# First query tile left unscaled in a hybrid layer's attention part

## The reference

```python
def _rmsnorm(t, w):
    inv = jax.lax.rsqrt(jnp.mean(tf * tf, axis=-1, keepdims=True) + EPS)
    return (tf * inv * w).astype(t.dtype)
q = (x @ Wq.T).reshape(b, s, H, HD).transpose(0, 2, 1, 3)      # H = 32, HD = 128
k = (x @ Wk.T).reshape(b, s, HKV, HD).transpose(0, 2, 1, 3)    # HKV = 8, so 4 query heads share a key head
v = (x @ Wv.T).reshape(b, s, HKV, HD).transpose(0, 2, 1, 3)
q = _rmsnorm(q, q_norm_w); k = _rmsnorm(k, k_norm_w)
scores = jnp.einsum('bkgqd,bksd->bkgqs', qg, k) / math.sqrt(HD)
bias = jnp.where(rel > 0, NEG_INF, slopes[:, :, None, None] * rel)
attn = jax.nn.softmax(scores + bias[None], axis=-1)
out = jnp.einsum('bkgqs,bksd->bkgqd', attn, v)
return out.transpose(0, 2, 1, 3).reshape(b, s, H * HD) @ Wo.T
```

## Time and profile before

| | us |
|---|---|
| median of 3 runs | 2434.09 |
| lowest, highest | 2433.47, 2441.58 |
| the profiled execution | 2437.14 |
| its span, first to last instruction | 2435.8 |
| TensorE busy in the span | 2373.6 (97%) |
| VectorE, ScalarE, GpSimd busy | 1646.2, 1189.8, 800.6 |

### The profile page before, as it was taken

How to read it: one execution, slowest core, us unless ns; L and a number is a source line. 1 busy time by engine, 2 the same in 40 slices (tenths; PEclk the granted TensorE clock), 3 DMA queues, 4 the chain that set the end, 5 groups by cost and what they waited for, 6 DMA issues and landing times.

```text
span 2435.8 us, 40875 instructions
## 1 busy us (share of the span) xinstructions
PE 2373.6 (97%) x12810; PEld 2020.9 (83%) x12810; DVE 1646.2 (68%) x3961; ACT 1189.8 (49%) x3788; POOL 800.6 (33%) x1204
## 2 busy tenths in 40 slices
PE   6899999999999999999999999999999989999999
PEld 4577777788888888988989889889898878888887
DVE  7666664534277877777777777777777776565553
ACT  6433332233256666666666666666666562222112
POOL 5530343212034344444443444444434350011000
PEclk9899999999999999999999999999999999999999
DMA  4235458987830634535346335344462306555554
GB/s 144 98 134 188 185 206 293 347 334 285 313 122 31 259 118 158 213 147 198 151 173 231 121 153 212 143 183 173 169 238 92 113 19 232 195 208 185 193 193 156
DMA packets 86579, 444.85 MB, mean 183 GB/s; under 512 B 9496, under 2 KB 16664, under 8 KB 66656
## 3 DMA queue, kind: packets, MB, share of 16 engines
q1 hardware_dynamic: 85008, 440.78, 48.5%
q10 hardware_dynamic: 1360, 1.46, 0.2%
HBM read 342.59 MB, written 99.61 MB: 182 GB/s over the span
## 4 chain that ended last, share of the span: by engine, by line
PE 82%; DMA 7%; DVE 4%; POOL 3%; ACT 2%; issue 2%; SPq 0%; ACTq 0%; POOLq 0%; DVEq 0%
PE psum L801 70%; DMA stage<-in_wqkv 3%; PE psum L2639 3%; PE psum L2615 2%; DMA weff_s<-short_st 1%; DMA weff_q<-q_parts 1%; POOL rr L2414 1%; PE psum L2633 1%; POOL prob L2446 1%; PE psum L1793 1%; DVE cc L2489 1%; PE psum L1814 1%; POOL srstd L1184 1%; PE psum L1826 1%; ACT prob L2388 1%
## 5 line engine op out<-in xcount | busy, mean ns | idle before, releaser
L801 PE MATMUL psum<-qw,xs 128*128 128x384 f32 x2688 | 512.0, 340 | 1.7 <-DMA xs<-weff_x 1.7
L801 PEld LDWEIGHTS psum<-qw,xs 128*128 128x128 f32 x2688 | 462.3, 189 | 2.5 <-DMA xs<-weff_x 1.9
L2446 POOL TENSOR_SCALAR prob<-prob,rsum 128x128 f32<-128x128 f32 (+1 forms) x512 | 231.6, 468 | 613.3 <-DVE rsum L2548 608.2
L2388 ACT ACTIVATE prob<-biased,nmax 128x256 f32<-128x256 f32 (+1 forms) x512 | 227.3, 447 | 125.8 <-DVE nmax L2538 125.8
L801 PE MATMUL psum<-wo_h,oT_h 128*128 128x512 f32 x512 | 214.3, 419 | 0.2
L801 PE MATMUL psum<-wo_h,oT_l 128*128 128x512 f32 x512 | 202.7, 396 | 0.0
L801 PE MATMUL psum<-wo_l,oT_h 128*128 128x512 f32 x512 | 202.5, 395 | 0.0
L2334 ACT ACTIVATE squares<-cc 128x128 f32<-128x128 f32 x512 | 152.6, 302 | 52.6 <-DVE cc L2468 49.6
L2489 DVE TENSOR_TENSOR cc<-cc,rr 128x512 f32<-128x512 f32 x64 | 97.7, 1526 | 102.3 <-POOL rr L2414 102.3
L2414 POOL TENSOR_TENSOR rr<-ss,mneg_half 128x6 f32<-128x6 f32 (+1 forms) x128 | 150.3, 1174 | 10.7
L801 PE MATMUL psum<-xT0h,wgu 128*128 128x512 f32 x448 | 152.1, 399 | 0.0
(11 more groups left out here) (338 smaller groups left out, 5903.0 us busy)
## 6 DMA issues: line engine op xcount, KB each, us to landing
xs<-weff_x SPq DMA_DIRECT2D x62, 1792.0 KB, 7.9
wgu<-weff_gu SPq DMA_DIRECT2D x42, 1024.0 KB, 7.9
weff_q<-q_parts SPq DMA_DIRECT2D x56, 768.0 KB, 3.6
qw<-weff_q SPq DMA_DIRECT2D x56, 768.0 KB, 8.0
wD<-weff_dn SPq DMA_DIRECT2D x56, 512.0 KB, 4.7
wS<-weff_s SPq DMA_DIRECT2D x28, 1024.0 KB, 7.0
wdn<-weff_dn SPq DMA_DIRECT2D x42, 512.0 KB, 4.1
weff_gu<-wgu SPq DMA_DIRECT2D x14, 1024.0 KB, 4.2
```

Source lines behind the costliest of these rows:

```text
L801: ins = pe.matmul(out_ap, stat[a], mov[b], start=start and n == 0, stop=stop and n == last)
L2388: act.activation(prob[:, b, lo:hi], biased[:, b % 2, lo:hi], ACT.Exp, bias=nmax[:, b, t:t + 1], scale=-1.0, accum_out=esum[:, b, t:t + 1]) ...
L2446: pool.tensor_scalar(prob[:, b, lo:hi], prob[:, b, lo:hi], rsum[:, b, t:t + 1], 1.0, ALU.mult, ALU.mult).then_inc(prob_done, 1)
```

## The change

Query tile 0 is no longer multiplied by its inverse roots. `qT0` transposes it as it comes from the sums, right behind `at1` and ahead of `outa1`, and waits for `c12` alone. Its scores are then too large by 1/r for each row. The bias step makes up for it. With s the unscaled scores and b the bias it forms b/r + s, and multiplies that by -r in the step that takes the least value, which gives -(b + r s). For this GpSimd makes two small tiles after tile 0's inverse roots: `q_root` (the mean square times the inverse root, so 1/r) and `q_neg` (-r). `low_bias` (L2537) becomes a scalar_tensor_tensor, and the low part's reduction (L2541) takes its factor from `q_neg` and not from a constant. Tile 1 is scaled as before, but its step `qsc1` comes ahead of `nrm0` on GpSimd. ScalarE's and VectorE's steps for k, q and v are put in another order. The diff, cut:

```diff
-            o.add(("nrm", 0, 0), "pool", 1.3, [("sqr", 0, 3), ("nrm", 0, 1)], 7)
+            o.add(("nrm", 0, 0), "pool", 1.7, [("sqr", 0, 3), ("qsc", 0, 1)], 7)
             o.add(("ksc", 0, 0), "act", 0.5, [("nrm", 0, 1)], 7)
-            o.add(("qsc", 0, 1), "pool", 1.05, [("nrm", 0, 0)], 7)
-            o.add(("qsc", 0, 0), "dve", 0.65, [("nrm", 0, 0)], 7)
+            o.add(("qsc", 0, 1), "pool", 1.05, [("nrm", 0, 1)], 7)
...
+        q_neg, q_root = sb2("q_neg", [P, GRP]), sb2("q_root", [P, GRP])
...
-            "pe": "... at1 set1 outa1 kT0 qT1 qT0 "
+            "pe": "... at1 set1 qT0 outa1 kT0 qT1 "
                   "out0 out1",
-            "dve": ... "pTlo3 qsc0 oTlo1 set1 vlo0 qTlo1 qTlo0 kTlo0 oadd0 oadd1",
+            "dve": ... "pTlo3 oTlo1 set1 qTlo0 vlo0 kTlo0 qTlo1 oadd0 oadd1",
-            "act": "... sqr3 ksc0 oThi1 vhi0 set1 qThi1 kThi0 qThi0",
+            "act": "... sqr3 ksc0 oThi1 set1 qThi0 vhi0 kThi0 qThi1",
-            "pool": "set0 norm0 norm1 sums norm2 norm3 nrm1 nrm0 qsc1 set1",
+            "pool": "set0 norm0 norm1 sums norm2 norm3 nrm1 qsc1 nrm0 set1",
...
                 pool.tensor_tensor(rr[:, part], ss[:, part], mneg_half[:, 0:part.stop - part.start],
-                                   ALU.pow).then_inc(r_done, 1)
+                                   ALU.pow).then_inc(r_done if b else r_part, 1)
+                if b == 0:
+                    if a:
+
+                        pool.wait_ge(biased_done, STILES * GRP * a)
+                    pool.wait_ge(r_part, 3 * a + 3)
+                    pool.tensor_tensor(q_root[:], ss[:, part], rr[:, part], ALU.mult).then_inc(r_done, 1)
+                    pool.tensor_scalar(q_neg[:], rr[:, part], -1.0, 1.0, ALU.mult, ALU.mult).then_inc(r_done, 1)
...
+                    dve.wait_ge(sq_done, squared(a - 1, 3))
...
-            elif what == "qsc" and b == 0:
-                dve.wait_ge(r_done, 2 * a + 2)
-                dve.tensor_tensor(q_heads(0), *q_scaled(0), ALU.mult).then_inc(q_sc0, 1)
...
-                    dve.tensor_tensor(low_bias[:, b % 2, :], psum[:, b, SC:SC + P], alibi[:, b, 0:P], ALU.add).then_inc(low_done, 1)
+                    if b == 0:
+                        dve.wait_ge(r_done, 3 * a + 3)
+                    dve.scalar_tensor_tensor(out=low_bias[:, b % 2, :], in0=alibi[:, b, 0:P], scalar=q_root[:, b:b + 1],
+                                             in1=psum[:, b, SC:SC + P], op0=ALU.mult, op1=ALU.add).then_inc(low_done, 1)
...
-                    dve.tensor_tensor_reduce(biased[:, b % 2, 0:P], psum[:, b, 0:P], low_bias[:, b % 2, :], -1.0, 3e38,
+                    dve.tensor_tensor_reduce(biased[:, b % 2, 0:P], psum[:, b, 0:P], low_bias[:, b % 2, :], q_neg[:, b:b + 1], 3e38,
                                              ALU.add, ALU.min, nmax[:, b, 0:1]).then_inc(biased_done, 1)
...
-                    pe.wait_ge(q_sc1 if b else q_sc0, a + 1)
+                    if b:
+                        pe.wait_ge(q_sc1, a + 1)
...
-                    pe.wait_ge(c_done, summed(a, "c12" if b else "c21"))
+                    pe.wait_ge(c_done, summed(a, "c12"))
```

More of the change, by code:

```diff
@@ L248, in hybrid_block @@
             "qkv_mm", "p1_done", "c_done", "sq_done", "r_part", "r_done", "v_hi", "v_lo", "k_sc", "kT_mm", "kT_hi", "kT_lo"))
-        q_sc0, q_sc1, qT_mm, qT_hi, qT_lo = (sem(n) for n in ("q_sc0", "q_sc1", "qT_mm", "qT_hi", "qT_lo"))
+        q_sc1, qT_mm, qT_hi, qT_lo = (sem(n) for n in ("q_sc1", "qT_mm", "qT_hi", "qT_lo"))
         sc_mm, biased_done, exp_done, rsum_done, prob_done = (sem(n) for n in (
@@ L2329, in act_projection @@
                 elif a:
-                    act.wait_ge(r_done, 2 * a)
+                    act.wait_ge(r_done, 3 * a)
                     act.wait_ge(sq_done, squared(a - 1, 3))
@@ L2345, in act_projection @@
             elif what == "ksc":
-                act.wait_ge(r_done, 2 * a + 1)
+                act.wait_ge(r_done, 3 * a + 1)
                 for t in range(STILES):
@@ L2406, in pool_projection @@
                 part = slice(0, SSQ[0]) if b else slice(SSQ[0], SSQ[0] + GRP)
-                n = 2 * a + 1 - b
                 pool.wait_ge(sq_done, squared(a, 4 if b else 3))
-                if a:
+                if a and b:
                     pool.wait_ge(k_sc, a)
-                    pool.wait_ge(q_sc0, a)
                 pool.tensor_scalar(ss[:, part], ss[:, part], 1.0, HD * RMS_EPS, ALU.mult, ALU.add).then_inc(r_part, 1)
-                pool.wait_ge(r_part, n + 1)
+                pool.wait_ge(r_part, 3 * a + 2 - b)
                 pool.tensor_tensor(rr[:, part], ss[:, part], mneg_half[:, 0:part.stop - part.start],
-                                   ALU.pow).then_inc(r_done, 1)
+                                   ALU.pow).then_inc(r_done if b else r_part, 1)
[5 more added lines that the diff above has]
+                    pool.tensor_scalar(q_neg[:], rr[:, part], -1.0, 1.0, ALU.mult, ALU.mult).then_inc(r_done, 1)
             elif what == "qsc" and b == 1:
-                pool.wait_ge(r_done, 2 * a + 1)
+                pool.wait_ge(r_done, 3 * a + 1)
                 pool.tensor_tensor(q_heads(1), *q_scaled(1), ALU.mult).then_inc(q_sc1, 1)
```

## The result

The changed kernel takes 2501.74 us (median of 4 runs, 2497.08 to 2506.55), the kernel before 2433.78 us (4 runs, 2430.67 to 2441.58) on the same chip. The ratio is 1.0277 with a 95% interval of 1.0262 to 1.0291: 2.8% slower, where 2422.0 us was forecast. The profiled execution took 2500.96 us, 63.8 more than that of before.

A forecast was written before the change was run, and what follows sets the result against it. TensorE, 97% busy, was taken as the bound, other engines counting only where it waits. Gains 7.5 + 3.8 + 1.8 less 1.0 made 12.1 us: 2434.1 to 2422.0 us, with 8 in 10 for 2412 to 2431.

The forecast's parts named there:

- the part on TensorE's order: Transposing tile 0 early: no new wait, switching costs nothing, `qTlo1` ends 1.4 us after the transposes, `sc0` starts at 2.8.
- R4: Rival, chance 0.05: bias steps with a scalar from a tile run like VectorE's slow form, 0.7 us per head; 2480.
- (a): TensorE's wait at `out0`, behind the transposes of k and q, for VectorE's `oTlo1`: 0.15 us x 50 units, 7.5 us gained.
- R3: Rival, chance 0.17: wait at `out0` only moves, since leaving transposes costs it anyway; 2429.5, or 2439 with a second exit.
- (c): TensorE between `sc0` and `sc1`, whose bank `oadd0` must have read: 0.07 us in every second unit, 1.8 us gained.
- (b): `sc0` waiting for `kTlo0`: 2.8 us gained in four layer norm units, 1.0 in two early ones, together 3.8.
- (d): Probabilities' transposes in 18 units where ScalarE's `qhi` waits for DMA, 13 late: bias steps cost 1.0 us, otherwise 0.
- R2: Rival, chance 0.15: units waiting for DMA win too, as the weight part's saving is issued up to 1.0 us earlier; 2415.3.
- ScalarE's wait for the saving: `qhi` waiting for a saved weight part: 0.8 to 1.0 us longer where it starts earlier, otherwise the same; start unmoved.
- Bias steps: VectorE's new bias forms: 0.08 us more per head (0 to 0.15), hidden in plain units, 1.0 us over 13 others.

The follow-up runs named there:

- the experiment with both counts right: Changed kernel with ScalarE's and VectorE's wait counts for query tile b both set to STILES * a + 1 + b: 2425.74 us, ratio 0.9957 to the kernel before.

## Why the prediction was wrong

The step that failed is in the part on TensorE's order: "`qThi1` is of the size of `oThi1` (0.60), `qTlo1` of that of `oTlo1` (0.68), so it ends some 1.4 us after the transposes, and `sc0` starts 2.8 us after them." It took for granted that each copy waits for its own tile's transposes, and so that only the last tile's two copies come behind them. By the unchanged counts both tiles' copies and v's and k's come behind them, one list after the other: `qTlo1` ended 4.09 us after them, counted from the start of `out0` as the 2.8 us are (1317.73 against 1313.64), and `sc0` was 1.30 us late in nearly every unit. No term of the sum stood for it, and among the rivals none was this mechanism; the slower one, R4, would have been 2480 for another reason.

Even with the counts right the 1.4 us were too few: 2.03 were measured in the same way (1293.80 against 1291.77), since `qTlo1` stands behind the three steps ahead of it on VectorE and not behind `qThi1` alone. That was covered.

The rest of the working, by the experiment with both counts right:

- (a), forecast -7.5, right. The wait for oT_l is gone and the stretch takes 0.68 us. R3 falls: leaving the transposes twice costs nothing.
- (a) and (c) together: 34 plain passes take 20.04 us on average, 20.25 before, so 0.21 each where 0.15 + 0.035 were forecast.
- (b), forecast -2.8 for the four layer norm units: 21.01, 20.96, 21.01 and 20.93 became 20.03, 20.01, 20.05 and 20.06, 3.8 less. These four are also among the 50 units of (a) and (c), at 0.185 each, so the sum had 3.5 for them: the size was right. The first seven passes together were 2.3 us shorter, but the very first alone varies from 21.6 to 24.0 over the kernels, and the six behind it gave 0.6 (126.4 to 125.8 us), less than (a) and (c) alone were to give there. No run shows the 1.0 for them.
- (d), forecast +1.0 for the bias steps and 0 for the rest: the 18 units took 375.0 us together and 373.8 after, and of the 1.2 us the five that were not late explain 5 x 0.21. The 13 others thus neither lost 1.0 nor won the 6.7 of R2, as far as single executions tell it: three kernels with the same plain pass took 370.6, 373.8 and 376.9 us for these 18 units, where R2 would make it about 368. The landing events of the trace show why: in the unit of 1393 us of that experiment the saving was issued at 1393.40, the load of `xs` ahead of it landed last at 1396.92, and the saving at 1398.79, 1.87 us later. Of the 24 savings that were issued while such a load was under way, none landed ahead of it: 1.85 to 2.42 us behind it in that experiment, 1.62 to 3.26 in the kernel before, with a median of 1.9 in both, though they were issued 5.7 us behind the load in the one and 6.6 in the other. In these traces the saving comes through behind the load; they thus agree with the rule of the Trainium skill (DMA: Bandwidth & Descriptors, section "Two DMAs through the same engine are not ordered") that was weighed in the prediction, which speaks of the order of the starts. That the landings keep the order too is what the traces add.
- ScalarE's wait for the saving was to be "longer by 0.8 to 1.0 us where it starts earlier or the same where not"; it grew from 48.5 us to 50.9 over 12, 0.2 each, about what (a) and (c) save in a unit. The wait takes up what was saved ahead of it, as the prediction had it, and only moving the reader (2412.23 us) took it off the path.
- Bias steps, forecast +0.08 us per head between 0 and 0.15: 0.11. R4 falls, and so does its reason: the 1.53 us of `qsc0` were for the most part a wait for GpSimd and no slow form of VectorE (last section).

With its terms the sum was 12.1 us, and 10.5 (7 to 15) were measured with the counts right. The sizes held, with some luck: the 1.0 us won in the first units and the 1.0 us lost in (d), which no run shows, cancel each other. What the working left out is the waits of the steps that changed places.

## What to carry to other kernels

When two producers of one semaphore change places, every count that waits on it has to be read again, on every engine down the chain, also where the diff doesn't touch that line: a count that is too high is still safe here and shows up only as time. A late step then starts exactly when a step it doesn't read has ended, and that is the sign to look for in a timeline. Where a slow transfer can't be sped up by an earlier issue, move the instruction that waits for it out of the queue's critical stretch.

## What the hardware showed that was not expected

GpSimd's small multiplication of two tiles, 128x4, takes 0.20 us or five times as long, and what decides it is VectorE. Two units of the changed kernel:

```profile
1312.79 0.96 DVE L896 TENSOR_TENSOR q_parts<-qt,q_parts 128x768 fp32r<-128x768 f32 x1
...
1312.84 0.97 POOL L2420 TENSOR_TENSOR q_root<-ss,rr 128x4 f32<-128x4 f32 x1
...
1355.77 0.20 POOL L2420 TENSOR_TENSOR q_root<-ss,rr 128x4 f32<-128x4 f32 x1
```

In 24 of the 64 units VectorE's split of a weight part (L896), which reads two tiles in SBUF, starts just ahead of `q_root`. There `q_root` takes 0.97 to 0.99 us and ends 0.06 us behind VectorE's step, each time. In 7 units it starts while VectorE makes `alibi`, also from two tiles in SBUF, takes 0.45 us and ends 0.06 us behind the step under way. In the 33 others it takes 0.20 us. In 24 of those units, with both counts right, VectorE is in the middle of `qTlo0`, which reads PSUM, and GpSimd isn't held up.

It works the other way too. In the kernel before, GpSimd's `qsc1` runs beside the start of `qsc0` (1319.52, 1.53 us long):

```profile
1319.45 1.05 POOL L2418 TENSOR_TENSOR cc<-cc,rr 128x512 f32<-128x512 f32 x1
```

In all 64 units `qsc0` starts 0.06 to 0.07 us behind `qsc1` and ends 0.55 us behind its end; `oTlo1`, with as many columns, takes 0.68 us. No unit has `qsc0` without `qsc1` beside it, but the first part of the same kernel has a shape of which some are alone: 32 steps of VectorE multiply two tiles of 128x256 there (`buf_c`). 20 of them take 0.39 to 0.43 us. 12 start in the middle of a GpSimd step on tiles as wide; they take 0.58 to 0.96 us and end 0.28 us behind it, each time:

```profile
172.07 1.09 POOL L1192 TENSOR_TENSOR buf_b<-buf_e,rot 128x256 f32<-128x256 f32 x1 [2.48 <-ACT buf_e L1340]
...
172.49 0.95 DVE L1638 TENSOR_TENSOR buf_c<-buf_e,rot 128x256 f32<-128x256 f32 x1
```

So about 1 us of the 1.53 us of `qsc0` was a wait for GpSimd, which the profile shows as busy time. The traces show which steps hold each other up; why isn't shown. `q_root`'s 0.97 us was covered here, since GpSimd's next step is almost 6 us away.
